# Another order of small steps on four engines in a linear-attention kernel: residual ahead of power and tree, statistics of two pairs on ScalarE, coefficients one period sooner, last three pairs reordered

## The reference

```python
x1 = group_norm_32(x)                       # groups of two channels, no weights
xn = group_norm(x1, gn1_w, gn1_b, 32)
qkv = einsum('oc,bchw->bohw', qkv_w, xn) + qkv_b          # 3 x 128 channels
q, k, v = split(qkv);  8 heads of 16 channels;  q = q * 16**-0.5
q_norm = softmax(q, over the 256 pixels)
k_norm = softmax(k, over the 16 channels of a head)
context = einsum('bhdn,bhen->bhde', k_norm, v)
out = einsum('bhde,bhdn->bhen', context, q_norm)
out = einsum('oc,bchw->bohw', out_w, out) + out_b
out = group_norm(out, gn2_w, gn2_b, 1)      # over all 64 channels and pixels
return x + (out + x1)
```

## Time and profile before

| | |
|---|---|
| three runs | 56.52 us median, 56.21 lowest, 59.24 highest |
| profiled execution | 56.09 us |
| its span, first to last instruction | 54.3 us |
| mean granted TensorE clock | 0.976 |
| PE busy | 44.1 us (81%), 439 matmuls |
| DVE busy | 42.0 us (77%), 145 instructions |
| ScalarE busy | 28.3 us (52%), 88 instructions |
| GpSimd busy | 25.6 us (47%), 55 instructions |
| load of pairs 4 to 7 | 512 KB in one DMA, 5.5 us from issue to landing |

### The profile page before, as it was taken

How to read it: one execution, slowest core, us unless ns; L and a number is a source line. 1 busy time by engine, 2 the same in 40 slices (tenths; PEclk the granted TensorE clock), 3 DMA queues, 4 the chain that set the end, 5 groups by cost and what they waited for, 6 DMA issues and landing times.

```text
span 54.3 us, 1401 instructions
## 1 busy us (share of the span) xinstructions
PE 44.1 (81%) x439; PEld 29.5 (54%) x439; DVE 42.0 (77%) x145; ACT 28.3 (52%) x88; POOL 25.6 (47%) x55
## 2 busy tenths in 40 slices
PE   2998779994999999599599979979997979895200
PEld 2775258743667665456475764656665754762200
DVE  0048996999999999899999599599686799355640
ACT  0713000079660523994797949677393480768500
POOL 5000404848660068957827916944877920040700
PEclk9999999999999999999999999999999999999955
DMA  0698950000000000000020020011003000002222
GB/s 0 152 280 285 334 206 1 0 0 0 0 0 0 18 0 0 0 0 0 0 97 12 6 97 0 0 43 54 6 0 103 6 6 0 0 0 97 97 97 97
DMA packets 2823, 2.84 MB, mean 52 GB/s; under 512 B 256, under 2 KB 2816, under 8 KB 2816
## 3 DMA queue, kind: packets, MB, share of 16 engines
q1 hardware_dynamic: 2528, 2.49, 14.1%
q10 hardware_dynamic: 288, 0.27, 1.5%
HBM read 1.71 MB, written 1.05 MB: 51 GB/s over the span
## 4 chain that ended last, share of the span: by engine, by line
DVE 32%; PE 31%; issue 13%; ACT 7%; POOL 6%; DMA 5%; ACTq 1%; DVEq 1%; POOLq 0%
PE kv_ps L430 7%; DMA brow<-b_qkv_dram 5%; PE o_ps L485 5%; DVE kmx L677 4%; PE q_ps L449 3%; DVE xstat L579 3%; POOL tree L241 3%; DVE vs L717 3%; PE o_ps L508 3%; DVE ek L685 3%; DVE rks L702 2%; DVE res L778 2%; DVE nqmax L694 2%; PE q_ps L446 2%; DVE ctxm L736 2%
## 5 line engine op out<-in xcount | busy, mean ns | idle before, releaser
L263 POOL TENSOR_TENSOR orstd<-ve,minus_half 128x1 f32<-128x1 f32 x8 | 4.4, 552 | 9.9 <-DVE ve L760 9.9
L317 ACT ACTIVATE ek<-ek 128x512 f32<-128x512 f32 x8 | 5.0, 627 | 7.1 <-DVE ek L685 7.1
L327 ACT ACTIVATE eq<-q_ps,nqmax 128x256 f32<-128x256 f32 x16 | 7.4, 473 | 1.9 <-DVE nqmax L694 1.9
L430 PE MATMUL kv_ps<-w_all,xn 64*128 64x256 f32 x64 | 8.3, 378 | 0.0
L241 POOL TENSOR_TENSOR tree<-ek 128x256 f32<-128x256 f32 x7 | 5.1, 730 | 6.7 <-ACT ek L317 6.7
L395 PE MATMUL kv_ps<-ones 128*128 128x512 f32 x16 | 6.0, 515 | 1.0 <-POOL ones L210 1.0
L430 PEld LDWEIGHTS kv_ps<-w_all,xn 64*128 64x128 f32 x64 | 6.0, 186 | 1.1 <-issue 0.4
L351 ACT ACTIVATE osq<-o_ps,nb 128x256 f32<-128x256 f32 x7 | 3.3, 473 | 6.3 <-DVE nb L751 3.2
L694 DVE TENSOR_REDUCE nqmax<-q_ps 128x2 f32<-128x512 f32 x8 | 5.4, 681 | 0.7 <-PE q_ps L449 0.7
L778 DVE SCALAR_TENSOR_TENSOR res<-oc,coef_o,skip 128x256 f32<-128x256 f32 x8 | 4.4, 548 | 2.0 <-issue 1.9
L717 DVE TENSOR_TENSOR vs<-kv_ps,rks 128x512 f32<-128x512 f32 x8 | 5.5, 692 | 0.3
(11 more groups left out here) (83 smaller groups left out, 84.3 us busy)
## 6 DMA issues: line engine op xcount, KB each, us to landing
out_dram<-res SPq DMA_DIRECT2D x8, 128.0 KB, 1.7
x_sb<-x_dram SPq DMA_DIRECT2D x1, 512.0 KB, 5.5
x_sb<-x_dram SPq DMA_DIRECT2D x2, 128.0 KB, 2.6
x_sb<-x_dram SPq DMA_DIRECT2D x1, 256.0 KB, 4.3
w_all<-weights_dram SPq DMA_DIRECT2D x1, 224.0 KB, 4.7
brow<-b_qkv_dram ACTq DMA_DIRECT2D x1, 192.0 KB, 3.0
mats<-matrices_dram SPq DMA_DIRECT2D x1, 160.0 KB, 5.5
par_avg<-params_dram ACTq DMA_DIRECT2D x1, 67.0 KB, 2.7
```

Source lines behind the costliest of these rows:

```text
L327: last = nc.scalar.activation(eq[:, p % 3, image, :], q_ps[:, image, 0, :], ACT.Exp, bias=nqmax[:, r, image:image + 1], accum_out=qs[:, p ...
L430: ins = nc.tensor.matmul(kv_ps[r][:, image, chunk, :, :, :], xn[rows(image), r, chunk * 128:(chunk + 1) * 128], w_f[rows(image), KV], star ...
```

## The change

- **GpSimd.** `first_key_sums` and `key_sums` are one function now. In periods 3 to 6 the order is residual of i − 3, power of i − 3, tree of i (it was power, first tree step, residual, rest of the tree). The residual of pair 4 comes ahead of its power. The power of the last group of pairs comes between the trees of pairs 1 and 2 (it was behind the tree of pair 2).
- **Statistics of pairs 6 and 7 on ScalarE** (`raw_sums`): a copy with a sum, a scaling to the mean, a square of the difference with a sum, a scaling to the variance. DVE keeps pairs 0 to 5; pair 4's BN_STATS moves ahead of the first `kmx`, pair 5's to where pair 4's was, with the aggregates of 4 and 5 behind it.
- **The last group's coefficients.** Variance and `obc` stand ahead of `nqmax` of pair 1, `group_coefficients(2)` and the residual's coefficients in period 2 (variance was in period 2, both sets of coefficients in period 3). PE's `group_average(2)` moves ahead of the warm-up behind the second queries. ScalarE's `affine` of pair 4 is in period 2.
- **The last three pairs.** On DVE `rks` and `vs` of pair 6 come ahead of the last `nqmax`, and `nb` of pair 5 between `rks` and `vs` of pair 7. ScalarE copies the folds of pair 5 ahead of the last query exponentials and centres pair 5 right after its squares.
- **`ctxm` has two buffers**, so its wait for the folds is for those of two pairs before.
- **`WARM`** is (8, 4, 1, 4, 3, 2, 4) where it was (8, 4, 3, 4, 5, 6, 1).

```diff
-WARM = (8, 4, 3, 4, 5, 6, 1)
+SUMMED = 6
+WARM = (8, 4, 1, 4, 3, 2, 4)
...
-        ctxm = sb("ctxm", [HIDDEN, 2, TILE])
+        ctxm = sb("ctxm", [HIDDEN, 2, 2, TILE])
...
-            for p in range(3):
-                first_key_sums(p)
-                key_sums(p)
+            key_sums(0)
+            key_sums(1)
             group_rstd(2)
+            key_sums(2)
             for i in range(3, PAIRS - 1):
+                residual(i - 3)
                 gn2_scale(i - 3)
-                first_key_sums(i)
-                residual(i - 3)
                 key_sums(i)
+            residual(PAIRS - 4)
             gn2_scale(PAIRS - 4)
-            for p in range(PAIRS - 4, PAIRS):
+            for p in range(PAIRS - 3, PAIRS):
                 residual(p)
...
+            def raw_sums():
+                n = PAIRS - SUMMED
+                act.wait_ge(x_in[load_of(SUMMED)], DMA)
+                for k in range(n):
+                    nc.scalar.activation(osq[:, k, :], x_sb[:, SUMMED + k, :], ACT.Copy,
+                                         accum_out=xsum[:, 0, k:k + 1]).then_inc(xsum_ready, 1)
+                act.wait_ge(xsum_ready, n)
+                nc.scalar.activation(xmv[:, SUMMED:PAIRS, 0], xsum[:, 0, :], ACT.Copy,
+                                     scale=1.0 / PIX).then_inc(xmean_ready, 1)
+                act.wait_ge(xmean_ready, 1)
+                for k in range(n):
+                    nc.scalar.activation(oc[:, k, :], x_sb[:, SUMMED + k, :], ACT.Square,
+                                         bias=xmv[:, SUMMED + k, 0:1], scale=-1.0,
+                                         accum_out=xsum[:, 1, k:k + 1]).then_inc(xsq_ready, 1)
+                act.wait_ge(xsq_ready, n)
+                nc.scalar.activation(xmv[:, SUMMED:PAIRS, 1], xsum[:, 1, :], ACT.Copy,
+                                     scale=1.0 / PIX).then_inc(xvar_ready, 1)
...
             bias_high()
+            raw_sums()
             key_exp(0)
...
                 fold_copy(i - 2)
                 key_exp(i)
-                if i == 3:
-                    affine(4)
-                if i > 2:
-                    affine(i + 2)
+                affine(i + 2)
...
             key_exp(PAIRS - 1)
+            fold_copy(PAIRS - 3)
             query_exp(PAIRS - 1)
-            fold_copy(PAIRS - 3)
             squares(PAIRS - 3)
+            centred(PAIRS - 3)
             fold_copy(PAIRS - 2)
             fold_copy(PAIRS - 1)
-            centred(PAIRS - 3)
...
             queries(1)
+            group_average(2)
             warm_up(WARM[4], o_ps[0][:])
             bias(2)
             keys_values(2)
             context(0)
-            group_average(2)
...
-                wait(dve, fold_done, 2 * TILES * p)
-                nc.vector.tensor_tensor(ctxm[:], context_of(p),
+                wait(dve, fold_done, 2 * TILES * (p - 1))
+                nc.vector.tensor_tensor(ctxm[:, p % 2, :, :], context_of(p),
...
             query_max(0)
             key_max(1)
             key_shift(1)
-            raw_stats(4)
+            raw_stats(5)
+            channel_moments(2)
             key_norm(0)
             scale_values(0)
+            group_variance(2)
+            output_bias()
             query_max(1)
-            for p in range(5, PAIRS):
-                raw_stats(p)
-            channel_moments(2)
```

More of the change, by code:

```diff
@@ L73, in attention_kernel @@
         xmv = sb("xmv", [P, PAIRS, 2])
+        xsum = sb("xsum", [P, 2, PAIRS - SUMMED])
         dev = sb("dev", [P, PAIRS])
@@ L132, in attention_kernel @@
         xstat_ready, xmv_ready, gavg_done = sem("xstat_ready"), sem("xmv_ready"), sem("gavg_done")
+        xsum_ready, xmean_ready, xsq_ready, xvar_ready = (
+            sem("xsum_ready"), sem("xmean_ready"), sem("xsq_ready"), sem("xvar_ready"))
         dev_ready, dev2_ready, gvar_ready = sem("dev_ready"), sem("dev2_ready"), sem("gvar_ready")
@@ L233, in group_rstd, with key_sums @@
                                         ALU.pow).then_inc(rstd_ready, 1)
-            def first_key_sums(p):
+            def key_sums(p):
                 r = p % 2
@@ L241, in first_key_sums @@
                 nc.gpsimd.tensor_tensor(tree[:], e[:, :, 0:8], e[:, :, 8:16], ALU.add).then_inc(tree_step, 1)
-            def key_sums(p):
-                r = p % 2
                 pool.wait_ge(tree_step, 3 * p + 1)
@@ L401, in group_average @@
                 if g == 2:
+                    pe.wait_ge(xvar_ready, 1)
                     pe.wait_ge(pow_ready, 2)
@@ L484, in folds @@
                         part = slice(t * TILE, (t + 1) * TILE)
-                        nc.tensor.matmul(o_of(p)[part, folded(image)], ctxm[part, image, :], wo_sb[part, :],
+                        nc.tensor.matmul(o_of(p)[part, folded(image)], ctxm[part, p % 2, image, :], wo_sb[part, :],
                                          start=(image == 0), stop=True,
@@ L582, in channel_moments @@
                 a, b = GROUPED[g]
-                for p in range(a, b):
+                for p in range(a, min(b, SUMMED)):
                     dve.wait_ge(xstat_ready, p + 1)
@@ L591, in group_variance @@
                 dve.wait_ge(gavg_done, g + 1)
+                if b > SUMMED:
+                    dve.wait_ge(xvar_ready, 1)
                 nc.vector.tensor_tensor(dev[:, a:b], xmv[:, a:b, 0], avg[:, :, 0],
@@ L794, in _ @@
             prepare_weights()
+            raw_stats(4)
             key_max(0)
@@ L815, in _ @@
                 variance_eps(i - 3)
-                if i == 3:
-                    group_coefficients(2)
                 key_norm(i - 1)
@@ L820, in _ @@
                 if i == 2:
-                    group_variance(2)
-                    output_bias()
-                if i == 3:
+                    group_coefficients(2)
                     residual_coefficients()
@@ L834, in _ @@
             key_shift(PAIRS - 1)
-            query_max(PAIRS - 1)
             key_norm(PAIRS - 2)
             scale_values(PAIRS - 2)
+            query_max(PAIRS - 1)
             query_norm(PAIRS - 2)
@@ L840, in _ @@
             key_norm(PAIRS - 1)
+            minus_mean(PAIRS - 3)
             scale_values(PAIRS - 1)
             mask_context(PAIRS - 2)
-            minus_mean(PAIRS - 3)
             query_norm(PAIRS - 1)
```

## The result

The changed kernel takes 54.66 us (median of four runs, 54.59 to 54.78). Against the kernel before the ratio is 0.970 (95% interval 0.965 to 0.976): 3.0% faster, 1.7 us. Some executions of most kernels here, the one before included, come out 1 to 4 us longer; the ratios leave them out, medians and ranges do not, and so the median of 57.84 that the kernel before showed in this comparison is not to be set against 54.66. I had forecast 53.8, 4.8% off the median of 56.52 then known. The sign was right and the time lies in the range, but the gain is about six tenths of the one forecast: the profiled executions differ by 56.09 − 54.68 = 1.41 us where the sum said 2.39.

The account below looks back on a forecast made before the run. It took a 4.52 us ring from folds through exponential, tree, `skip`, `res`, `kmx`, `ctxm` as the bound. Gains 0.11 + 0.05 + 0.53 + 0.80 + 0.90 = 2.39 took 56.09 to 53.70, ordinarily 53.8; range 53.0 to 55.6.

Parts of the forecast that it names:

- The ring over `skip`: Steady periods: folds, fold copy, exponential, tree, `skip`, `res`, `kmx`, `ctxm`, folds; claimed to set the period at 4.52 us.
- PE's ring: Steady periods: folds, next keys and values projection, `kmx`, `ctxm`, folds; 4.25 us, claimed late next once `skip` is early.
- the term of 0.80: Steady periods: `skip` ahead of power and tree shortens three periods from 4.52 to 4.25, gain 0.80 us.
- Start: Statistics of pairs 6 and 7 on ScalarE, variance moved earlier: `kmx` of pair 2 0.11 us sooner, at 16.71.
- Coefficients: Last group's coefficient steps one period sooner, in period 2: `nb` of pair 0 at 20.80 instead of 20.96.
- Net −0.05: DVE in period 2: loses the 1.15 us variance, gets six coefficient steps; claimed 0.05 us less in all.
- Period 3: Main-loop pass 3, 4.93 us before; claimed 4.40 with coefficient work gone from DVE, gain 0.53 us.
- 22.39: Forecast time in us of the folds from which period 3 is counted, 22.55 before, so 0.16 sooner.
- End: Last three pairs: DVE's 0.72 us idle before the last `nqmax` filled, last folds' 0.18 wait gone; gain 0.90.
- The rival of the clock: Five fewer warm-ups let PE's clock fall to 0.50 between 7 and 15 us: +3.8, 57.6 us; chance 0.04.
- The sum: All gains over the whole kernel added: 2.39 us off the profiled 56.09.

Follow-up runs that it names:

- experiment 1: Kernel before with one edit: in periods 4 to 6 GpSimd's `skip` comes ahead of power and tree; 55.51 us, ratio 0.983.
- Experiment 4: Changed kernel with period 2's six DVE coefficient steps behind `nb` of pair 0 and ScalarE's `affine` behind the query exponentials; 53.98 us, ratio 0.956.
- experiment 5: Changed kernel with GpSimd's trees for pairs 1 and 2 cut to one of 32 groups in their first three steps; 54.11 us, ratio 0.957.
- experiment 2: Kernel before with only the new order of the last three pairs, two `ctxm` buffers and `WARM` (8, 4, 3, 4, 5, 2, 4); 55.32 us, ratio 0.981.
- experiment 8: Experiment 4's kernel, statistics of pairs 6 and 7 back on DVE, variance behind `nqmax` of pair 1, no warm-ups before keys of pair 2; 57.75 us.
- Experiment 10: Experiment 4's kernel with no warm-ups after the first twelve, `WARM` (8, 4, 0, 0, 0, 0, 0); 58.16 us.

## Why the prediction was right and wrong, point by point

- **What bounds the steady periods, and what is late next: right.** The ring over `skip` was read from two ends that meet (34.90 and 34.99) although the profile said "issue". PE's ring was added up as 4.25 and is 4.27; the term of 0.80 measured 0.75, of which experiment 1 has 0.66 alone.
- **Start: wrong, by 0.39.** The step that failed is "`kmx` of pair 2 starts 0.11 sooner, at 16.71". It started 0.28 later. The variance was priced at the 1.15 that it took in its old place; in its new place it took 16.14 − 14.65 = 1.49. Of the difference of 0.34, `dev` held by GpSimd is 0.28 and the idle spell in front of `nqmax`, with what goes with it, 0.29 (0.36 from `obc` to `nqmax` instead of 0.07); the old place had a wait of 0.23 of its own, at `pow_in`. ScalarE's sums were priced well: by ACT's timeline of the changed kernel they end at 10.5, before the exponential at 10.96.

```profile
10.32 0.20 ACT L320 ACTIVATE xmv<-xsum 128x2 f32<-128x2 f32 x1
10.96 0.63 ACT L338 ACTIVATE ek<-ek 128x512 f32<-128x512 f32 x1 [0.44 <-DVE ek L707]
```

- **Coefficients: wrong, by a further 0.29.** "Net −0.05" was +0.24: the six steps took 20.88 − 19.49 = 1.39, not 1.10, as GpSimd's tree stood beside them. The rows warned of it. `mean_r` at 24.35 with 0.58 stood in the earlier trace rows, four times its like, and I took it over as the price of the step without asking what it was waiting for. It ends at 24.93, and this tree step of before, not among my rows, at 24.90:

```profile
24.18 0.72 POOL L241 TENSOR_TENSOR tree<-ek 128x256 f32<-128x256 f32 x1 [0.67 <-ACT ek L317]
```

The term was not only mis-sized: the six steps were put ahead of `nb`, the instruction that the next folds hang on, and beside a tree, and I counted them as neutral there because the variance had gone. Experiment 4 shows that this place costs 0.7, and experiment 5 that nearly all of it is the waiting for GpSimd there.
- **Period 3: right** (4.42 for 4.40). So the forecast "22.39" for the folds of pair 1 failed by 0.68 only through the `nb` before it.
- **End: right in the mechanism, 0.2 short.** 0.90 forecast, 0.97 in experiment 2, 0.69 in the changed kernel, the difference being the idle spell before `nb` of pair 5. The step that failed is that `nb` of pair 5 "sits in the latency between `rks` and `vs`: 0". In experiment 2 it holds (`rks` to `vs` 0.39, before 0.38); in the changed kernel it is 0.68, because the idle spell of 0.22 falls there, which no row of before could have told.
- **The rival of the clock** got 0.04, and the changed kernel keeps 1.00 to the end of PE's work. Yet it is near: fourteen more warm-ups taken out bring it about, and so does experiment 8, with three fewer and a longer wait. That "a gap of a microsecond did not" take the clock down was no ground for calling it far. The Trainium skill (TensorE: Matmul & The Clock Gate, "A second HAM failure mode: psum-queue depth-cycling") has short idle spells between groups of matmuls make the clock swing. Experiment 10 agrees in that the clock first falls after spells of 0.50 and less; the changed kernel, with spells of 0.94 and its clock at 1.00, shows that such spells are not enough by themselves.
- **The sum:** 2.39 − 0.39 − 0.29 − 0.21 (end) − 0.05 (steady) − 0.02 (period 3) = 1.43, the 1.44 of the traces.

## What to carry to other kernels

When steps are moved, price them in the new neighbourhood. When a small DVE step lasts several times as long as its like, look for a GpSimd instruction that ends just before it does: in these traces that was what it waited for, and the price belongs to the place, not to the step. Within a period, put what nobody waits for behind the instruction that the other engines hang on. Matmuls in idle time are part of the kernel's speed, so take them out a few at a time and read the granted clock.

## What the runs showed that I had not expected

- A step of DVE on four elements (in each partition) can take 0.74 us: it ends only when GpSimd's running tree step has ended. Seen in before (0.58), after (0.44, 0.74, 0.43) and in experiment 4 (0.48), and taken away in experiment 5. Beside a power of one column it was not seen.
- DVE idles 0.2 us with no releaser at two instructions of the changed kernel, and six memsets in an idle stretch at the start make both spells vanish and the kernel 0.4 us faster. The place in the instruction stream decides; the cause is open, and so is whether the spells account for all of the 0.4.
- PE's granted clock fell to 0.50 with 14 warm-ups fewer, and stayed down while PE was fully busy: 3 us longer between the lowest times, 4 us between the medians. What exactly takes it down is open.
